# Order and grouping of the first loads of a recurrent two-layer kernel, with the wait ahead of stage one split up

## The reference

```python
xn = _layernorm(x)
s = _L0_attn_ref(xn, ...)          # 2 transformer layers, 2 heads, rotary factors, softmax over 256 keys
g = _silu(_L0_ffn_ref(xn, ...))    # 64 experts, top 8, at most 64 tokens each, and a shared expert
x = x + s * g
xn = _layernorm(x)
s = _L1_attn_ref(xn, ...)          # linear attention, 16 heads of 8
g = _silu(_L1_ffn_ref(xn, ...))    # 32 experts, top 1, and a shared expert
x = x + s * g
```

## Time and profile before

| | us |
|---|---|
| median of 3 runs | 1456.67 (1455.31 to 1457.17) |
| profiled execution, its time | 1457.29 |
| profiled execution, span from first to last instruction | 1455.5 |
| mean granted TensorE clock, share of full speed | 0.923 |
| PE busy in the span | 1217.5 (84%) |
| DVE busy | 1018.3 (70%) |
| ACT busy | 783.6 (54%) |
| POOL busy | 653.9 (45%) |

### The profile page before, as it was taken

How to read it: one execution, slowest core, us unless ns; L and a number is a source line. 1 busy time by engine, 2 the same in 40 slices (tenths; PEclk the granted TensorE clock), 3 DMA queues, 4 the chain that set the end, 5 groups by cost and what they waited for, 6 DMA issues and landing times. The chain is left out here.

```text
span 1455.5 us, 29222 instructions
## 1 busy us (share of the span) xinstructions
PE 1217.5 (84%) x7815; PEld 920.2 (63%) x7816; DVE 1018.3 (70%) x3639; ACT 783.6 (54%) x2010; POOL 653.9 (45%) x1270
## 2 busy tenths in 40 slices
PE   3999999999935999999999555588888888599993
PEld 2778787777724677777777444356666666366662
DVE  2777777777777677777776388667777777266663
ACT  1675756566622656656566366556666666233331
POOL 2343434344221555545555378614444444146665
PEclk9999999999967999999999755589999999799997
DMA  3424333333311222222222166534444444355562
GB/s 138 152 93 141 100 132 115 116 130 101 115 42 30 41 60 47 54 58 41 58 47 49 35 191 215 166 111 151 148 147 149 148 148 140 110 154 175 176 181 71
DMA packets 159257, 162.84 MB, mean 112 GB/s; under 512 B 20950, under 2 KB 138429, under 8 KB 159216
## 3 DMA queue, kind: packets, MB, share of 16 engines
q1 hardware_dynamic: 143936, 133.23, 29.3%
q0 software_dynamic: 14848, 26.77, 6.7%
q10 hardware_dynamic: 432, 2.38, 0.4%
HBM read 76.59 MB, written 71.04 MB: 101 GB/s over the span
## 5 line engine op out<-in xcount | busy, mean ns | idle before, releaser
L392 ACT ACTIVATE pr<-ps,nmx 128x256 f32<-128x256 f32 x256 | 117.7, 472 | 44.6 <-DVE nmx L439 44.0
L380 ACT ACTIVATE big<-ps,BHS 128x256 f32<-128x256 f32 x256 | 107.0, 470 | 62.2 <-PE ps L257 61.5
L257 PE MATMUL ps<-big,W 128*128 128x256 f32 x512 | 131.8, 403 | 5.9 <-ACT big L385 5.9
L270 PE MATMUL ps<-W,big 128*128 128x128 f32 x1024 | 130.7, 281 | 0.0
L270 PEld LDWEIGHTS ps<-W,big 128*128 128x128 f32 x1024 | 119.6, 192 | 13.9 <-ACT big L380 9.9
L2144 POOL DMA_INDIRECT out<-X,io x96 | 100.4, 1046 | 34.4 <-issue 34.4
L257 PEld LDWEIGHTS ps<-big,W 128*128 128x128 f32 x512 | 96.4, 198 | 27.8 <-ACT big L385 16.3
L439 DVE TENSOR_REDUCE nmx<-ps 128x2 f32<-128x512 f32 x128 | 82.5, 686 | 39.6 <-PE ps L292 38.9
L1986 PE MATMUL ps<-big,zT 128*128 x192 | 101.9, 613 | 8.5 <-DVE pr L2082 8.3
L1007 POOL DMA_INDIRECT ffn<-big,si x64 | 94.0, 1468 | 26.6 <-issue 26.6
L2060 ACT ACTIVATE pr<-ps 128x256 f32<-128x256 f32 x96 | 36.8, 383 | 106.6 <-PE ps L1986 106.6
(11 more groups left out here) (256 smaller groups left out, 3302.4 us busy)
## 6 DMA issues: line engine op xcount, KB each, us to landing
srt<-big SPq DMA_DIRECT2D x16, 1584.0 KB, 5.8
X<-srt SPq DMA_DIRECT2D x24, 800.0 KB
big<-we SPq DMA_DIRECT2D x16, 768.0 KB, 4.9
rowd<-big SPq DMA_DIRECT2D x32, 272.0 KB, 2.2
big<-x SPq DMA_DIRECT2D x64, 128.0 KB, 2.2
X<-big SPq DMA_DIRECT2D x64, 128.0 KB, 2.1
big<-we SPq DMA_DIRECT2D x16, 384.0 KB, 3.6
X<-srt SPq DMA_DIRECT2D x24, 256.0 KB, 3.0
```

Of the source, the lines that this page charges most:

```text
L257: last = pe.matmul(pb[2 * g + f // 2][:, f % 2 * S:(f % 2 + 1) * S], W0[:, l, 512 + f * P:512 + (f + 1) * P], zT2[:, g, :], start=True, st ...
L270: last = pe.matmul(pb[4 + g][:, t * C:(t + 1) * C], hT[:, g, f, t * P:(t + 1) * P], W0[:, l, 1024 + f * C:1024 + (f + 1) * C], start=(f == ...
L380: act.activation(hT[:, g, f, :], pb[2 * g + half][:, f % 2 * S:(f % 2 + 1) * S], ACT.Silu, bias=BHS[:, l, f:f + 1], scale=GELU).then_inc(s ...
L392: last = act.activation(pr[:, g, h, t, :], pb[2 * g + h][:, t * S:(t + 1) * S], ACT.Exp, bias=nmx[:, g, h * TPU + t:h * TPU + t + 1], accu ...
```

## The change

The first block now issues the DMAs in another order and grouping, no engine waits in it, and the preparation on DVE is moved into stage one.

- SP issues first the two `xin` loads, then `COL`, `WS`, `ROT`, `ROW`, `WSD`, and last `W1`.
- ACT issues the identity (the first 128 columns of `CST`, 64 KB), then `W0`'s first half, then the other 1097 columns of `CST` (548.5 KB), then `W0`'s second half. `W1` has moved from ACT's queue to SP's.
- The semaphore `ld_first` counts `COL` and the identity. `ld_w` counts six loads: `WS`, `ROT`, `ROW`, `WSD`, `W0`'s first half and the rest of `CST`.
- In stage one PE waits for `ld_first` before its first transposes and for `ld_w` before the first logits; ACT waits for `ld_first` before its first copy; DVE does the statistics of turn 0, waits for both semaphores, and then does the six preparing instructions.

```diff
--- before.py
+++ after.py
@@ -171,25 +171,26 @@
             return bass.ds(TPU * i + HT * g, TPU)
 
 
-        ld_small, ld_w, ld_late, zeroed = sem("ld_small"), sem("ld_w"), sem("ld_late"), sem("zeroed")
+        ld_first, ld_w, ld_late, zeroed = sem("ld_first"), sem("ld_w"), sem("ld_late"), sem("zeroed")
         in_sem = [sem(f"s1_xin{g}") for g in range(2)]
         zero = early([P, ROWW])
+        N_LD = 6
         with nc.Block() as block:
             @block.sync
             def _(sp):
-                for dst, src in ((COL, cols), (CST, cst), (ROW, rows), (ROT, rot), (WS, ws), (WSD, wsd)):
-                    sp.dma_start(dst[:, :], src).then_inc(ld_small, 16)
                 for g in range(2):
                     sp.dma_start(xin[:, g, :, :], x_t[:, HT * g:HT * g + TPU, :]).then_inc(in_sem[g], 16)
-                sp.wait_ge(ld_small, 6 * 16)
-                sp.wait_ge(ld_w, 16)
+                sp.dma_start(COL[:, :], cols).then_inc(ld_first, 16)
+                for dst, src in ((WS, ws), (ROT, rot), (ROW, rows), (WSD, wsd)):
+                    sp.dma_start(dst[:, :], src).then_inc(ld_w, 16)
+                sp.dma_start(W1[:, :], w1).then_inc(ld_late, 16)
 
             @block.scalar
             def _(act):
+                act.dma_start(CST[:, 0:C_BLK], cst[:, 0:C_BLK]).then_inc(ld_first, 16)
                 act.dma_start(W0[:, 0, :], w0[:, 0:1536]).then_inc(ld_w, 16)
-
+                act.dma_start(CST[:, C_BLK:], cst[:, C_BLK:]).then_inc(ld_w, 16)
                 act.dma_start(W0[:, 1, :], w0[:, 1536:3072]).then_inc(ld_late, 16)
-                act.dma_start(W1[:, :], w1).then_inc(ld_late, 16)
 
             @block.gpsimd
             def _(pool):
@@ -199,20 +200,6 @@
                 pool.memset(MHALF4[:, :], -0.5)
                 pool.memset(EPS4[:, :], EPS)
                 pool.memset(PHALF[:, :], 0.5)
-
-            @block.vector
-            def _(dve):
-                dve.wait_ge(ld_small, 6 * 16)
-                dve.tensor_copy(TRI[:, :], CST[:, C_TRI:C_TRI + P])
-                dve.tensor_copy(ONES[:, :], CST[:, C_ONE:C_ONE + P])
-                dve.tensor_copy(SUM[:, :], CST[:, C_SUM:C_SUM + P // 16])
-                for l in range(DEPTH):
-                    dve.tensor_scalar(BHS[:, l, :], COL[:, l * NCOL + BH:l * NCOL + BH + FC], GELU, None, ALU.mult)
-
-                dve.wait_ge(ld_w, 16)
-                dve.tensor_scalar(W0[:, 0, 1024:1536], W0[:, 0, 1024:1536], 1.0 / GELU, None, ALU.mult)
-
-
 
         LAYER = ["stats1", "z1", "zT1", "xl1", "qkv", "qk_sb", "scores", "mx", "probs", "pT", "pT_sb",
                  "pv", "attT", "wo", "stats2", "z2", "zT2", "xl2", "hid", "hT", "y", "xout"]
@@ -798,7 +785,9 @@
                                                      xnT[:, g, t * P:(t + 1) * P], WS[:, 0:E0], start=True, stop=True)
                             last.then_inc(s["logits"], 1)
 
+                    pe.wait_ge(ld_first, 32)
                     x.front(pe, 0)
+                    pe.wait_ge(ld_w, N_LD * 16)
                     x.logits(pe, 0)
                     bodies(pe, lambda i, att=True, ffn=True, front=True: body_tensor(pe, s, i, 0, att, ffn, x))
 
@@ -848,6 +837,7 @@
                                 act.wait_ge(s["key"], i)
                             act.activation(lg[:, :, :, :].rearrange("p g t e -> p (g t e)"), pb[6][:, 0:2 * TPU * E0],
                                            ACT.Copy).then_inc(s["lg"], 1)
+                    act.wait_ge(ld_first, 32)
                     x.front(act, 0)
                     x.logits(act, 0)
                     bodies(act, lambda i, att=True, ffn=True, front=True: body_scalar(act, s, i, 0, att, ffn, x))
@@ -910,6 +900,14 @@
 
                     dve.memset(rsm[:, :, :, :], 1.0).then_inc(s["xout"], 2)
                     x.stats(dve, 0)
+                    dve.wait_ge(ld_w, N_LD * 16)
+                    dve.wait_ge(ld_first, 32)
+                    dve.tensor_copy(TRI[:, :], CST[:, C_TRI:C_TRI + P])
+                    dve.tensor_copy(ONES[:, :], CST[:, C_ONE:C_ONE + P])
+                    dve.tensor_copy(SUM[:, :], CST[:, C_SUM:C_SUM + P // 16])
+                    for l in range(DEPTH):
+                        dve.tensor_scalar(BHS[:, l, :], COL[:, l * NCOL + BH:l * NCOL + BH + FC], GELU, None, ALU.mult)
+                    dve.tensor_scalar(W0[:, 0, 1024:1536], W0[:, 0, 1024:1536], 1.0 / GELU, None, ALU.mult)
 
                     def between():
                         dve.wait_ge(s["keyT"], HALF)
```

## The result

| | before | changed |
|---|---|---|
| median of 7 runs, us | 1456.20 | 1449.88 |
| lowest to highest, us | 1454.90 to 1459.51 | 1445.36 to 1452.00 |
| profiled execution's span, us | 1455.5 | 1444.9 |

The ratio is 0.9949, 95% interval 0.9933 to 0.9965: the kernel became faster by 0.51%, or 7.4 us (5.1 to 9.8), and the medians differ by 6.3. The forecast was 1452.8 us in a range of 1449.0 to 1455.9, which holds the measured time by 0.9 us, but its gain of 3.9 us is only about half of what came. That the range holds it is luck: it reaches so low only for rival A, and the range of the forecast itself ended at 1450.0.

The account below looks back on a forecast made before the run. The prediction took a chain of engines to bound the kernel, its first link a load, with nothing computing for 13.18 us. Gain 5.15 less table load 1.28 is 3.87 us, so median 1452.8 us, range 1449.0 to 1455.9.

Parts of the forecast that it names:

- rival A: Start: x comes much earlier and the barrier sets the start; gain 7.2 us, 1449.4 us, chance 0.14.
- 1: First block: without a wait the barrier opens at 5.5 and the memset is over at 5.6 us.
- 2: First loads: queues alternate row by row, x is whole at 9.35 us, statistics start then instead of 14.50; gain 5.15 us.
- 3: ACT's table load moves behind the wait for PE's first transposes, onto the path; loss 1.28 us.
- 4: PE's waits for `ld_first` and `ld_w` in stage one stay hidden by more than 4.8 us.
- 5: DVE's six preparing instructions, 0.91 us, now follow the loads at 12 to 14, hidden by 8 us; cost 0.
- 6: SP's and POOL's queues: `W1` moves to the end of SP's, POOL issues nothing here; cost 0.
- 7: PE's slow start and later granted clock may shift by 1 us either way; taken as 0.
- C: First loads: x lands hardly earlier than before; at worst 1457.4 us, chance 0.10.
- B: Stage one: the table load is not on the path; gain 5.15 us, 1451.5 us, chance 0.06.
- D: The start gains and later parts give back 1 to 3 us; 1455.5 us, chance 0.07.
- E: Turn 0: the 1.3 us pause keeps PE at lower speed, so slower by 1.1 to 7.8 us, 1461.1 us, chance 0.05.

Follow-up runs that it names:

- the long load from the start: Changed kernel with ACT's first load made 16 unbroken rows of 5632 bytes per DMA engine, issued with the first x load; ratio 0.9940.
- the combination: Changed kernel with x's loads first in two queues, other loads issued inside stage one, no ACT wait for ld_first, preparation behind z1; 1448.03 us, ratio 0.9906.
- the split alone: Changed kernel with the loads in the order and grouping of before, so only the common wait is gone; 1455.52 us, ratio 0.9999.
- the repetitions: The changed kernel run twice more, unchanged, against the kernel before; 1452.06 us, ratio 0.9935, and 1448.24 us, ratio 0.9957.
- the longer load: Changed kernel with ACT's second load, behind the identity, made 16 rows of 5632 bytes per DMA engine instead of 8 of 6144; ratio 0.9925.

## Where the prediction was right, and the step that failed

1. Barrier at 5.5, memset over at 5.6: the memset ran from 5.64 to 5.71. Right.
2. **x at 9.35: this term was mis-sized by 3 us, and it is the step that failed.** x landed at 6.3, outside the stated 7.5 to 9.6. The mechanism was right, one row against one row, as the long load from the start shows. Wrong was that both queues would hold rows all the time, and when x's rows start. The bound of 7.5 had the first point: 8 rows of x beside the identity and 8 free are the 16 rows for each engine of x's first load, and that load was through before ACT's long rows came. I took it for a bound and not for the forecast, and it is worth 1.85 of the 3.05 us. Neither forecast nor bound had the rest. By the working the first load would land at 3.5 + 0.21 + 0.42 = 4.1, and it landed at 3.5, which is 0.6. The last 0.6, an estimate by difference, falls in the place of eight rows of the rest of CST, 1.35 in the sum: there x's queue had three to four packets to one of ACT's. The reading is a pause of ACT's queue between its loads, and it stays a reading.
3. The table load on the path, 1.28: right. It was the price of ACT's redundant wait, and the first copy came 1.36 earlier without it. The drain of 1380 ns of the Trainium skill, ScalarE: Activation LUTs, section "What ACT_TABLE_LOAD costs", is not seen; the activation begins 0.02 us behind the load's end here too (14.24 + 1.28, then 15.54).
4. The waits for loads hidden: right for this change, by 4 us (12.15 against 16.34) instead of 4.8; false in the combination with the statistics at 3.66 and the weights issued later.
5. The preparation at cost 0: wrong by 0.28. DVE hid it, but POOL's work beside it was slowed, and POOL was on the path.
6. The queues of SP and POOL: right.
7. PE's speed: within its bound of 1. From the logits to q it took 0.11 longer than before, and 0.29 longer than in the kernel without ACT's wait; the other profiles don't tie that to the pause. The granted clock reads 1.00 all through this phase, from 22 to 27 us before and from 15 to 24 in the changed kernel. The fall of the granted clock later in turn 0 came out by execution. Against the kernel before, with its 3 us of it, none was worth 0.84 us of lead, and the longest took 1.46.

The sum of the terms as measured: 8.15 - 1.28 - 0.28 - 0.11 = 6.48; the remaining 0.16 up to the 6.32 at q lies in small gaps between POOL, PE and ACT. The interval of the timed gain, 5.1 to 9.8, holds that.

Of the rivals, A named nearly this landing (6.0 to 6.4) by a mechanism that the runs refute. C is what the split alone is. B, D and E did not come, and E's mechanism, PE slower for the pause, isn't shown even in small.

Open stays whether the change is worth about 1 us more than the 6.3 at q, as the 7.4 of the ratio and 8.8 and 7.2 of the medians in the repetitions may suggest. The experiments point the same way: in each of the thirteen experiments the difference of the medians is larger than the lead at q, by 0.35 to 4.1 us, even for the split alone (0.55 slower by the medians, 1.26 later at q). There is one profile of the kernel before, so it can't be told whether its q came early in that execution or whether a later part of it differs.

## What to carry to other kernels

Order of loads and granularity of waits are worth something only together: give the first-needed load the front of a queue and let its reader wait for it alone, then look at what is waited for next. Before adding a wait, ask whether another engine's wait already orders it, and look at the built order: a second wait on ACT can move ahead of a table load and expose it. Where two queues run at once, a load of short rows should be issued so far ahead that its rows pass before the other queue's long rows begin, since side by side each short row waited for a long one here.

## What the runs showed of the hardware that was not expected

- While both queues hold rows they alternate one for one, at unequal sizes too: 33 to 36, 32 to 31 and 34 to 36 packets in three half microseconds, with 512 bytes against 5632, and 10 to 10 with 88 bytes against 6144.
- x's second load landed near 6.3 in the changed kernel and near 3.9 with ACT's long load issued half a microsecond later. With x's second load and ACT's long load issued within some 0.05 us of each other, either could reach the engines first (5, 11 and 26 packets of x's queue from 3.0 to 3.5 us in the changed kernel, 99 with the longer load). What decides that wasn't found.
- DVE's six preparing instructions made two POOL instructions on other tiles take 1.16 instead of 0.88 us.
- With the granted clock at 1.00, PE's product group before q took 0.69 to 1.06 us and the one after it 1.03 to 1.91, and neither went by the pause of 1.3 us ahead of them.
- In the same stretch of the same kernel the granted clock was 1.00 in one execution and 0.56 in another.
